# Adjacency attention in split fp16: from one Strassen-Winograd unit per pair of row blocks to two

## The reference

```python
h = relu(layernorm(x))
q = h @ Wq.T + bq;  k = key @ Wk.T + bk;  v = value @ Wv.T + bv
s = (q @ k.T) / 64 * adj                  # adj is 0 or 1
s = where(abs(s) < 1e-5, -1e9, s)
out = x + (softmax(s) @ v) @ Wm.T + bm
```

## Time and profile before

| | |
|---|---|
| median of three runs | 1566.84 us |
| the profiled execution | 1566.73 us, of it span 1564.9 us |
| busy: PE, DVE, ACT, GpSimd | 1541.6, 1105.6, 625.0, 223.4 us |
| granted TensorE clock | 1.000 |
| DMA: moved, share of 16 engines | 260.60 MB, 66.6% in the hardware queue |
| transfers: adjacency tile, factor, P transpose | 256 of 256 KB, 98 of 512 KB, 252; 2.9, 4.0, 3.2 us to landing (median) |

### The profile page before, as it was taken

The page is one execution under the profiler, slowest core; times in us unless marked ns, Lnnn a source line. Parts: engine busy times, 40 slices in busy tenths (PEclk is TensorE's granted clock), DMA queues, the critical chain, the costliest instruction groups (busy, mean ns, idle before and its releaser), DMA issues.

```text
span 1564.9 us, 24177 instructions
## 1 busy us (share of the span) xinstructions
PE 1541.6 (99%) x7134; PEld 707.1 (45%) x7134; DVE 1105.6 (71%) x2444; ACT 625.0 (40%) x1009; POOL 223.4 (14%) x285
## 2 busy tenths in 40 slices
PE   8998999999999999999999999999999999999998
PEld 5543444444444444444444444444444444444444
DVE  5989887767667676767767666776766667676652
ACT  5776343333334333343333333433333333333332
POOL 5162002011020101102010010201001020200100
PEclk9999999999999999999999999999999999999999
DMA  9824768667675765758576575766658576665754
GB/s 347 272 75 99 180 153 204 165 153 178 141 201 141 181 162 145 189 134 203 145 179 167 130 203 133 201 147 173 165 131 207 130 202 151 163 165 141 185 112 108
DMA packets 449149, 260.60 MB, mean 167 GB/s; under 512 B 376531, under 2 KB 380883, under 8 KB 448982
## 3 DMA queue, kind: packets, MB, share of 16 engines
q1 hardware_dynamic: 449104, 260.12, 66.6%
q10 hardware_dynamic: 6, 0.01, 0.0%
HBM read 156.51 MB, written 12.06 MB: 108 GB/s over the span
## 4 chain that ended last, share of the span: by engine, by line
PE 90%; DVE 5%; issue 2%; DMA 1%; ACT 1%; SPq 0%; DVEq 0%; ACTq 0%
PE R L738 14%; PE R L740 14%; PE R L739 14%; PE S L740 11%; PE S L738 11%; PE S L739 11%; PE M L738 3%; PE M L740 3%; PE M L739 3%; DMA pT<-ph 1%; DVE Zbuf L1550 1%; PE R L809 1%; DVE Zbuf L1472 1%; PE R L855 1%; DVE small L1226 1%
## 5 line engine op out<-in xcount | busy, mean ns | idle before, releaser
L1177 ACT ACTIVATE drop<-Zbuf 128x512 f32<-128x512 f32 x256 | 161.2, 630 | 737.8 <-DVE cmx L1472 644.2
L738 PE MATMUL R<-Vbuf,pT 128*128 128x512 f16 x1008 | 382.1, 379 | 7.4 <-DMA pT<-ph 4.9
L740 PE MATMUL R<-Vbuf,pT 128*128 128x512 f16 x1008 | 382.0, 379 | 0.0
L739 PE MATMUL R<-Vbuf,pT 128*128 128x512 f16 x1008 | 382.0, 379 | 0.0
L738 PE MATMUL S<-Kbuf,qT 128*128 128x512 f16 x856 | 324.5, 379 | 0.0
L739 PE MATMUL S<-Kbuf,qT 128*128 128x512 f16 x856 | 324.4, 379 | 0.0
L740 PE MATMUL S<-Kbuf,qT 128*128 128x512 f16 x856 | 324.4, 379 | 0.0
L1519 DVE SCALAR_TENSOR_TENSOR Zbuf<-S,rs,adjb 128x512 f32<-128x512 f32 x214 | 160.2, 749 | 217.6 <-PE S L740 211.9
L1472 DVE CUSTOM_DVE_ANT_0 Zbuf<-drop,Zbuf 128x512 f32<-128x512 f32 x256 | 190.5, 744 | 0.0
L1572 DVE TENSOR_SCALAR drop<-drop,rs 128x512 f32<-128x512 f32 x256 | 145.9, 570 | 27.2 <-ACT drop L1177 25.0
L1183 ACT ACTIVATE Zbuf<-Zbuf,smx 128x1024 f32<-128x1024 f32 x128 | 157.4, 1230 | 5.3 <-DVE smx L1486 2.5
(11 more groups left out here) (251 smaller groups left out, 1628.6 us busy)
## 6 DMA issues: line engine op xcount, KB each, us to landing
adjb<-in_adj_dram SPq DMA_DIRECT2D x256, 256.0 KB, 2.9
Kbuf<-key_factors SPq DMA_DIRECT2D x98, 512.0 KB, 4.0
xq<-in_x_dram SPq DMA_DIRECT2D x32, 256.0 KB, 2.8
Kbuf<-in_L_gnn_key_dram SPq DMA_DIRECT2D x8, 1024.0 KB, 13.6
xr<-in_x_dram SPq DMA_DIRECT2D x32, 256.0 KB, 2.7
out_dram<-xr SPq DMA_DIRECT2D x31, 256.0 KB, 2.5
Vbuf<-in_L_gnn_value_dram SPq DMA_DIRECT2D x7, 1024.0 KB, 7.4
pT<-ph SPq DMA_TRANSPOSE x130, 3.2
```

Source lines behind the costliest of these rows:

```text
L738: nc.tensor.matmul(ps, lhs[0], rhs[0], start=start, stop=False, skip_group_check=added)
L739: nc.tensor.matmul(ps, lhs[0], rhs[1], start=False, stop=False, skip_group_check=added)
L740: return nc.tensor.matmul(ps, lhs[1], rhs[0], start=False, stop=stop, skip_group_check=added)
L1177: nc.scalar.activation(drop[:, :], tile_of(s.i, s.j), ACT.Abs).then_inc(abs_ready, 1)
```

## The change

Two units for each pair: `UNITS` = key groups (5, 4) and (7, 6). They start with the fourth pair instead of the third (`FIRST` = 4), and pair 4 is written out as well.

- **Order.** Group orders become 0 1 2 3 5 4 7 6 and 4 5 6 7 0 1 2 3. Units 0 and 1 of the first block stand in steps 4, 5, of the second in 6, 7; units 2 and 3 in steps 8, 9 and 10, 11. The late products of the first block go into W[0], of the second into S[1].
- **Factors.** Fourteen, in 16 pieces over steps 19 to 50. Kbuf keeps groups 0 to 3; the other four are eight slots: four for B11 and T2 of both blocks, loaded once (steps 42 to 48), three as a ring (`RING_Q` = 4, 5, 6), one for the mixes of the rows (qS). Ten loads a pair: B21 (of block 1, that is the second) in step 5; T1 and B22 of it in 6; T3 of block 0 in 7, T4 of block 0 at the end of 7 in SP's order; T3 of block 1 in 8, T4 of it in 9; B21, T1, B22 of block 0 for the next pair in 12, 13, 14.
- **Rows.** The mixes move to steps 1 (GpSimd), 2 (ACT), 3 (DVE). The preparation of a row block no longer counts `pc`: `projected`, PE's projection with DVE's row scales, stands in c = 7 instead of c = 0, the units of the row in j = 0 and 12, the halves of q in j = 0 and 9 instead of c = 1.

```diff
-        FIRST_ORDER, SECOND_ORDER = [0, 1, 2, 3, 4, 5, 7, 6], [6, 7, 0, 1, 2, 3, 4, 5]
-        ONE, TWO = 7, 6
+        FIRST_ORDER, SECOND_ORDER = [0, 1, 2, 3, 5, 4, 7, 6], [4, 5, 6, 7, 0, 1, 2, 3]
+        UNIT, NU, MAKE_STEP, FIRST = 4, len(UNITS), 19, 4
+        RING_Q, MIX_Q = (4, 5, 6), 7
...
+                self.stats = row_at(0, self.c == 5)
+                self.halves_h = row_at(1, self.c == 6)
+                self.turned = row_at(2, self.c == 7)
+                self.projected = row_at(3, self.c == 7)
+                self.scaled = row_at(4, j in (0, NC + 4))
+                self.halves_q = row_at(5, j in (0, NC + 1))
...
@@ SP, step
-                if s.unit == 0:
-                    wait(sp, unit_mm, s.unit_before + 1)
-                    load_factor("B22", 0)
-                    wait(sp, unit_mm, s.unit_before + 2)
-                    load_factor("T3", 1)
-                if s.unit == 1:
-                    wait(sp, scores_done, s.t)
-                    load_factor("T4", 2)
+                if s.strassen and s.j == 5:
+                    wait(sp, scores_done, s.t)
+                    load_factor((1, "B21"), 4)
+                if s.strassen and s.j == 6:
+                    wait(sp, unit_mm, 6 * s.nth + 3)
+                    load_factor((1, "T1"), 5)
+                    wait(sp, scores_done, s.t)
+                    load_factor((1, "B22"), 6)
+                if s.strassen and s.j == 7:
+                    wait(sp, scores_done, s.t)
+                    load_factor((0, "T3"), 4)
+                if s.strassen and s.j == 8:
+                    wait(sp, scores_done, s.t)
+                    load_factor((1, "T3"), 6)
+                if s.strassen and s.j == 9:
+                    wait(sp, scores_done, s.t)
+                    load_factor((1, "T4"), 4)
...
+                if s.strassen and s.j == 7:
+                    wait(sp, unit_mm, 6 * s.nth + 6)
+                    load_factor((0, "T4"), 5)
+                if s.prefetch and s.j in (12, 13, 14):
+                    wait(sp, scores_done, s.t)
+                    load_factor((0, ("B21", "T1", "B22")[s.j - 12]), RING_Q[s.j - 12])
...
@@ PE, step
-                        unit_product(W[0], qT[:, 1, :, 2:4, :], 2, False).then_inc(scores_done, 1)
+                        if s.w == 0:
+                            wait(pe, kr_in[5], 48 * s.nth + 48)
+                        else:
+                            wait(pe, kr_in[4], 64 * s.nth + 64)
+                        unit_product((W[0], S[1])[s.w], qT[:, 1, :, 2:4, :], (5, 4)[s.w], False).then_inc(scores_done, 1)
...
-                if s.pc == 3 and s.has_prep:
+                if s.projected is not None:
...
-                    project_q(s.n, s.n - 4)
+                    project_q(s.projected, s.projected - 4)
...
@@ ACT, step
                 if s.unit == 0:
-                    wait(act, unit_mm, s.unit_before + 1)
-                    wait(act, s_made, s.i - 1)
-                    nc.scalar.activation(SUM_U, S[s.j % 2][:, :], ACT.Copy).then_inc(p1_ready, 1)
+                    wait(act, unit_mm, 6 * s.nth + 3 * s.w + 1)
+                    wait(act, p_lo, PASS * (s.i - 1) + NC + 2 * s.w + 2)
+                    nc.scalar.activation(SUM_U[s.w], S[s.j % 2][:, :], ACT.Copy).then_inc(p1_ready, 1)
...
@@ DVE, step
-                if s.pc == 3 and s.has_prep:
-                    row_scales(s.n, xq[:, :])
-                    row_mix(s.n, rstd[:, 1:2])
-                    row_units(s.n, 1 - s.p, 0, NPAIR, 2 * (s.n - 2))
+                if s.projected is not None:
+                    row_scales(s.projected, xq[:, :])
+                    row_mix(s.projected, rstd[:, 1:2])
+                if s.scaled is not None:
+                    row_units(s.scaled, 1 - s.p, 0, NPAIR, 2 * (s.scaled - 2))
```

More of the change, by code:

```diff
@@ L372, in __init__ @@
                 self.more_adj = not late or t + ADJ_SLOTS < STEPS
-                self.more_x = not late or self.pb + 1 < NB
+                self.more_x = self.halves_q is not None and (not late or self.halves_q < NB)
                 self.pair = NPAIR * 2 * i + (j - LAG_P) // 2
@@ L515, in step @@
                     load_adj(s.b + (s.c + ADJ_SLOTS) // NC, group_at(s.i, s.j + ADJ_SLOTS), s.j % ADJ_SLOTS)
[L516 removed]
+                if s.turned is not None and isinstance(s.t, int) and s.t < PASS:
                     h_T(s)
```

252 lines of the change are left out of this document (132 added, 120 removed).

## The result

| | before | after |
|---|---|---|
| median of four runs | 1566.39 us | 1597.1 us |
| from, to | 1564.79, 1566.91 | 1595.47, 1601.33 |
| ratio, 95% interval | | 1.0206 [1.0193, 1.0219] |
| profiled execution, span | 1566.73, 1564.9 | 1596.63, 1594.8 |

The change makes the kernel 30.7 us slower. I had forecast 6 us slower, 1572.8, and a range that ends at 1592.

A forecast was written before the change was run, and what follows sets the result against it. PE alone was taken as the bound. Waits of 1.9 us make a pair 92.55 against 92.17: +0.38 x 13 = +4.9, with the third pair's +1.1 +6.0, so 1572.8 us; range 1557 to 1592.

The forecast's parts named there:

- The rest: Extra loads, making factors to step 50 and kept loads: 0, at most 2 us in all, within DVE's idle time.
- What goes, 15.5 us: 72 score matmuls off PE at 0.2158 us each; 13 pairs fall to 420 matmuls, 90.65 us if nothing waits.
- The third pair's +1.1: The third pair goes from 426 to 432 matmuls and loses its wait: 93.2 against 92.17 us.
- Step 4, +0.6 per pair: The unit's third product waits for ACT's copy of the first, held up by the output row; 0.4 to 0.8.
- Step 9, +1.0 per pair: The product waits for the first unit's T4 load, with DVE's late tile 8 (0.6) inside; 0.6 to 2.1.
- Steps 10 and 11, +0.3 per pair: Step 11 waits for DVE's tile 10 or the second unit's T4 load; 0 to 1.1.
- rival 3: DMA queue fills up in steps 7 to 11, transposes of P come late: 3.7 per pair, 1595 us; chance 0.13.
- the low ends: Waits of 1.0 to 1.2 us per pair give -4.5 to -3 us, 1563.
- Rival 1: Not slower: cover removes a wait at step 4 or 9; 1556 us with one left, 1548 with none; chance 0.17.

The follow-up runs named there:

- g4_t3: f3_together plus T4 of the second unit ahead of step 8's transpose, halves of q in step 10, T3 of the first unit at the end of step 6; 1565.46 us.
- e4_stages_old: The changed kernel with projection, units and halves of q back in their old places (c = 0 and 1) for the first 42 to 48 steps; 1591.73 us.
- e3_sums_early: The changed kernel with DVE's sum of the exponentials one step earlier, in steps 2 and 10; 1591.21 us.
- e1_t4_first: The changed kernel with the load for step 9 (T4 of the first unit) ahead of step 7's transpose in SP's queue; 1592.86 us.
- h2_both_t4: The changed kernel with both T4 loads issued early, in steps 7 and 8, and nothing else; 1589.03 us.
- f2_light_late: e1_t4_first with DVE's tiles of units 2 and 3 leaving out the adjacency multiplication, a price and not a version; 1585.74 us.
- g2_first5: The changed kernel with units from the fifth pair on, kept and ring loads 16 steps later; 1591.09 us.
- f3_together: The changed kernel with e1_t4_first's and e4_stages_old's edits, first row's projection in step 8 from step 42 on, sums early for the first row block alone; 1581.91 us.
- h1: g4_t3 with units from the fifth pair on; 1561.19 us, ratio 0.9971 to the kernel before.

## Why the prediction was wrong

The sign and the mechanisms were right: slower, by waits at steps 4, 9 and 11 that a DMA, DVE and ACT end. The size was not, 6 forecast against 30.7. The largest part of the miss is "The rest" (the making of the factors, put at 0 to 2 us), then the steady pairs, above all steps 10 and 11, then the last pair taken for a steady one. Step by step:

- **What goes, 15.5 us.** Right: with the waits gone (g4_t3) a pair of 420 matmuls takes 91.45, with a loss of 0.3 to 1.0 in step 10 in seven of ten and one of 0.3 to 1.3 in step 11 in three, against 90.65 if nothing waited: 0.75 of waits on average, so the removed matmuls are worth their pitch. The third pair's +1.1 is right too (93.24 in e4_stages_old).
- **Step 4, +0.6 per pair.** Right: 0.58, and 0.59 by its removal (e3_sums_early).
- **Step 9, +1.0 per pair.** Right in mechanism, 0.25 short in size. In the profile after, the offsets from step 7's start (759.38) are: tile 7 at +4.8, row scales +8.25, tile 8 done +12.4 (forecast 12.2), load issued +8.51 (8.51), product at +12.73 (12.65). And DVE's lateness inside the load's was 0.86 from start to start (e1_t4_first), forecast 0.6. The mean of 1.25 is the load's: it landed 4.1 to 4.5 us after its issue over the steady pairs, mean 4.34, and the forecast took 4.1. The Trainium skill's price for a transfer (SBUF — State Buffer, "The DMA setup-cost knee"), an estimated 3.2 us, would have taken the load's row out of step 9; it stands there in all 13 pairs.
- **Steps 10 and 11, +0.3 per pair.** The failed term of the steady pair: 0.4 at the scores and 0.4 at P, about 0.75. The forecast set DVE (done at +19.8) and T4 of the second unit (20.2 to 21.4) against a start of +20.4, and took 0.3 between 0 and 1.1. Two things were mis-sized. DVE has tile 10 done at 779.19 + 1.02 = 780.21, which is +20.8, 1.0 later than forecast and no longer ahead of the start: it begins tile 8 0.2 late, its six pieces for tile 8 take 4.1 instead of 3.7 (the row's small maxima alone 0.78), those for tile 9 4.0, with short idle times between them, and tile 10's two 1.8 instead of 1.5, since the xr add holds the multiply for 1.02 instead of 0.69 (this was in the working). The load is issued at +16.6 (775.98), forecast +16.2. And that P's transpose would also be late in these short steps was in rival 3 only. DVE's +20.8 is the same in ten of the eleven steady pairs and is the floor of the wait; the load lands between +20.4 and +21.4 and sets it where it is later. h2_both_t4 and f2_light_late show the load and DVE each with its share.
- Together 2.6 of waits per pair instead of 1.9, a steady pair +1.1 instead of +0.38: 8 us of the miss (eleven pairs, 12.3 against 4.2).
- **"The rest", making the factors: "0, at most 2 us in all".** The step that failed outright: 6.0 in pair 3 and about 5.3 in pair 4 (98.53 less a steady 93.29), 11 us. I argued from an old trace "with the same work in pairs 2 and 3" that had no wait. The trace gave less cover than that: one of the waits of the earlier trace rows falls in step 21, among the pieces (steps 19 to 34), and DVE waited for ACT's part of a piece five times, 3.8 us at the longest. Whether the making is what made that transpose late, no run shows. PE in before:

```profile
174.22 0.39 PE L738 MATMUL R<-Vbuf,pT 128*128 128x512 f16 x1 [1.50 <-DMA pT<-ph]
```

Elsewhere the old order had room for DVE's stalls; the new one does not. In pair 3 the change puts the projection into the very step in which h is transposed, one step of 5.2 us after the row on DVE that making delays; before, a full step lay between. e4_stages_old puts that step back, together with the units and halves of q, and the 6.0 are gone. In pair 4 the making of the last pieces now overlaps units (before, the first unit came in step 38, after the last piece in 34); g2_first5 parts them and the 5.2 are gone. The forecast has the making "to step 50", the first unit begins in step 52, and it took these as if they did not touch; the first loads (from step 48 on) and DVE's lateness reach over.
- **The last pair costed like the others.** +3.8 instead of +0.4. It has no projection in step 7, so step 9 comes 2.6 us sooner and the load, still behind a transpose, is 4.3 late instead of 1; e1_t4_first takes 4.9 us off.
- The misses add up: 8.1 in the steady pairs, 6.0 in pair 3, 6.0 in pair 4 (6.4 less 0.4), 3.4 in the last and 0.3 ahead of pair 3, 23.8 of 23.9 (spans, 29.9 less 6.0). One sum in the range was also off: waits of 1.0 a pair, the low ends, give 13 x (91.65 - 92.17) + 1.1 = -5.7, not -4.5; it changes nothing here.
- **Rivals.** Rival 3 named the time, 1595, for a wrong reason: the queue's bandwidth. That it lies near the 1597 measured is luck. Its sign, a late transpose of P, is there in small part (0.4 a pair where it had 3.7), and P's transposes took 3.3 us median to landing between 640 and 1380 us, not 5 (3.2 before; one of 5.9 stands in pair 4). And from f3_together to g4_t3 the same bytes move, two loads and the halves of q change places, and 16.4 us go. Rival 1 needed "one of the two waits gone"; both had to go, and the ones at 8, 10 and 11.

What is not settled: how pair 4's 5.3 divide between the first loads and the units; and the steady loss at `osb`'s transpose in g4 and h1 (step 10, 0.3 to 1.1 in seven of ten pairs), which no run tried to remove, so that the queue's load as its cause is not ruled out.

## What to carry to other kernels

When an edit shortens steps or moves a stage, cost the steps at the seams (where a preparation still runs, the first unit, the last pair, which lacks a neighbour that gave cover) one by one; here they held 17 of 30 us, and a trace without waits only vouches for its own order. Waits in consecutive short steps are layers: removing the one that shows pays only down to the next (e1: 0 a pair; f3, with three edits that act there: 0.4; g4, with all: 1.8), so test an order with all of them off before judging it. Where one queue issues everything in program order, as SP's does here, check a load's place before its bytes: two loads and the halves of q moved, 16.4 us gone, the same 283.25 MB.
